# Output projection as three rounded passes with channels in partitions, in a fused attention and expert layer on one Trainium2 core

## The reference

```
x = x + attn(layernorm(x))
x = x + moe(layernorm(x))
```

## Time and profile before

| | |
|---|---|
| median of 3 runs | 872.1 us (870.09 to 872.9) |
| the profiled execution | 868.56 us |
| its span, first to last instruction | 866.8 us |
| mean granted TensorE clock | 0.997 |
| TensorE matmul busy | 846.0 us (98% of the span) |
| VectorE / ScalarE / GpSimd busy | 620.2 / 625.7 / 572.4 us |
| output projection on TensorE, 512 rows | 69.4 us |

### The profile page before, as it was taken

How to read it: one execution, slowest core, us unless ns; L and a number is a source line. 1 busy time by engine, 2 the same in 40 slices (tenths; PEclk the granted TensorE clock), 3 DMA queues, 4 the chain that set the end, 5 groups by cost and what they waited for, 6 DMA issues and landing times.

```text
span 866.8 us, 20127 instructions
## 1 busy us (share of the span) xinstructions
PE 846.0 (98%) x6535; PEld 670.2 (77%) x6535; DVE 620.2 (72%) x2348; ACT 625.7 (72%) x1639; POOL 572.4 (66%) x522
## 2 busy tenths in 40 slices
PE   8999999999999999999999999999998999999995
PEld 4677777777777777777777777777767999988884
DVE  6677787887777777878778778788787665545442
ACT  5877777877787777778877778777796776555552
POOL 5475576578657956775787569666748667555664
PEclk9999999999999999999999999999999999999998
DMA  7575550000000000000000000000011344333342
GB/s 197 207 285 211 235 161 2 1 26 8 7 8 26 1 7 9 24 8 1 21 13 7 5 29 1 8 7 26 8 26 44 48 56 67 44 51 48 50 53 26
DMA packets 44038, 44.69 MB, mean 52 GB/s; under 512 B 4112, under 2 KB 36240, under 8 KB 43936
## 3 DMA queue, kind: packets, MB, share of 16 engines
q0 software_dynamic: 16528, 26.03, 12.4%
q1 hardware_dynamic: 27120, 17.25, 7.1%
q10 hardware_dynamic: 288, 0.13, 0.1%
HBM read 15.28 MB, written 28.12 MB: 50 GB/s over the span
## 4 chain that ended last, share of the span: by engine, by line
PE 88%; DVE 4%; POOL 3%; issue 2%; ACT 2%; POOLq 0%; DVEq 0%; ACTq 0%
PE low_ps L1322 12%; PE low_ps L1309 9%; PE mid_ps L1244 7%; PE mid_ps L1246 7%; PE mid_ps L1245 7%; PE out_ps L1333 7%; PE top_ps L1309 7%; PE mid_ps L1295 6%; PE low_ps L1295 4%; PE low_ps L1534 4%; PE top_ps L1295 4%; POOL prob L408 2%; DVE prob L847 2%; PE out_ps L1509 2%; PE top_ps L1244 2%; PE top_ps L1246 2%
## 5 line engine op out<-in xcount | busy, mean ns | idle before, releaser
L408 POOL TENSOR_TENSOR prob<-prob,row_inv 128x512 f32<-128x512 f32 (+3 forms) x256 | 318.7, 1264 | 200.2 <-DVE row_inv L854 199.8
L588 ACT ACTIVATE prob<-prob,neg_max 128x256 f32<-128x256 f32 (+3 forms) x512 | 280.6, 550 | 7.8 <-DVE neg_max L847 0.9
L1322 PE MATMUL low_ps<-PT,v_sb 128*64 128x512 f32 (+3 forms) x1024 | 152.0, 439 | 0.3 <-ACT PT L594 0.3
L1322 PEld LDWEIGHTS low_ps<-PT,v_sb 128*64 128x64 f32 x1024 | 68.1, 136 | 92.1 <-issue 65.2
L859 DVE COPY PT<-low_ps 128x512 f32<-128x512 f32 (+1 forms) x128 | 104.1, 814 | 16.0 <-PE low_ps L1309 13.5
L599 ACT ACTIVATE v_sb<-mid_ps 128x512 f32<-128x512 f32 x64 | 38.3, 598 | 94.0 <-PE mid_ps L1246 93.8
L1160 DVE TENSOR_TENSOR prob<-mid_ps,prob 128x512 f32<-128x512 f32 x71 | 49.0, 691 | 78.1 <-PE mid_ps L1246 43.9
L847 DVE CUSTOM_DVE_ANT_0 prob<-mid_ps,mask 128x128 f32<-128x128 f32 (+1 forms) x256 | 93.5, 421 | 9.1 <-PE mid_ps L1295 4.9
L1309 PE MATMUL low_ps<-ident,prob 128*128 128x128 f32 x640 | 94.5, 278 | 2.0 <-POOL prob L408 0.5
L588 ACT ACTIVATION_READ_ACCUMULATOR prob<-prob,neg_max 128x1 f32 x512 | 95.7, 187 | 0.0
L594 ACT ACTIVATE PT<-top_ps 128x1024 f32<-128x1024 f32 x64 | 65.7, 1026 | 37.8 <-PE top_ps L1309 32.5
(11 more groups left out here) (253 smaller groups left out, 1872.2 us busy)
## 6 DMA issues: line engine op xcount, KB each, us to landing
routed_rows<-W_dn POOLq DMA_DIRECT2D x8, 2080.0 KB
X<-routed_rows SPq DMA_DIRECT2D x37, 65.0 KB
X<-routed_rows SPq DMA_DIRECT2D x17, 130.0 KB
X<-in_L_attn_x SPq DMA_DIRECT2D x8, 256.0 KB, 5.3
...
```

What stands on the lines that cost most here:

```text
L408: nc.gpsimd.tensor_tensor(p_pair(i), p_pair(i), row_inv[:, i, :].unsqueeze(2).to_broadcast([P, 2, P * (i + 1)]), ALU.mult).then_inc(S["nor ...
L588: nc.scalar.activation(p_at(i, h), p_at(i, h), ACT.Exp, bias=neg_max[:, i, h:h + 1], scale=-1.0, accum_out=row_sum[:, i, h:h + 1]).then_in ...
L1322: last = nc.tensor.matmul(y_ps[h * HD:(h + 1) * HD, j * P:T], v_sb[:, half, j, o + h * HD:o + (h + 1) * HD], PT[:, h, j, j:NT, :].rearrang ...
```

## The change

`project_out` turns its operands round. The weights are now a 128 x 128 piece of w_out and the moving operand is y with 512 tokens, so that out^T comes out with channels in partitions; and it is done in three rounded passes. For that:

- w_out is loaded into a buffer of its own and split once, near the start, into hi (ScalarE) and lo (VectorE).
- ScalarE's `y_copy` writes y's hi part, now between the two exponentials of block 3; VectorE makes the lo part (`y_lo`, new, one per step) after `t_copy(n, 1)`, which now stands ahead of `inv(n, 3)`; `project_out` waits for `y_lo_done`.
- Once a batch, ScalarE copies out^T (`post_out`, in k = 8), TensorE transposes it back in four products (`post_out`, in k = 1 of the next batch), and VectorE adds it to X from there (`post_x2`, now in k = 2).
- On VectorE, routing work changes places: `pre_stats` in k = 1 and `post_choose` in k = 5 go behind the step's last copy, `post_chosen` goes from behind it in k = 5 to ahead of `t_copy` in k = 6, and the cast to `row_i` goes from `post_weights` (k = 7) to `post_rows` (k = 6).
- At the end VectorE does `split_lo(4)`, `y_lo(63)`, `split_lo(2)`, `split_lo(6)`; `post_x2` of the last batch goes from `late(0)` to `late(1)`.
- Buffers: `y_sb`'s second use by the experts' part goes to `v_sb`, and the slots' weights and row numbers go to `wdT`.

```diff
-        Wo_sb = sb("Wo_sb", [P, NP, C])
+        Wo_sb = sb("Wo_sb", [P, 2, NP, C], F32R)
-        y_sb = sb("y_sb", [P, T])
+        y_sb = sb("y_sb", [P, T], F32R)
+        y_parts = [y_sb[:, :].rearrange("p (a n) -> p a n", a=2), xT_sb[:, 0, :, :]]
...
@@ ScalarE, step @@
-                    exps(n, 3)
+                    exp_head(n, 3, 0)
                 y_copy(n - 1)
+                if cur:
+                    exp_head(n, 3, 1)
...
+                if k == NP:
+                    post_out(n // NP - 1)
                 if cur:
                     t3_copy(n)
...
+            def post_out(b):
+                seen(act, S["out_ready"], NP * (b + 1))
+                seen(act, S["logits_ready"], b)
+                nc.scalar.activation(outT[:, :], out_ps[:, :], ACT.Copy).then_inc(S["outT_copied"], 1)
...
@@ VectorE @@
+            def y_lo(n):
+                seen(dve, S["y_copied"], n + 1)
+                seen(dve, S["out_ready"], n)
+                nc.vector.tensor_tensor(y_parts[1], y_ps.rearrange("p (a n) -> p a n", a=2), y_parts[0].bitcast(F32),
+                                        ALU.subtract).then_inc(S["y_lo_done"], 1)
...
-                if post is not None and k == 1:
+                if post is not None and k == 2:
                     post_x2(post)
-                if pre is not None and k == 1:
-                    pre_stats(pre)
...
-                if post is not None and k == 5:
-                    post_choose(post)
+                if post is not None and k == 6:
+                    post_chosen(post)
...
                 if cur:
+                    t_copy(n, 1)
+                y_lo(n - 1)
+                if cur:
                     inv(n, 3)
-                    t_copy(n, 1)
...
-            for e in (4, 2, 6):
+            split_lo(4)
+            y_lo(STEPS - 1)
+            for e in (2, 6):
                 split_lo(e)
...
@@ TensorE @@
             def project_out(n, pair):
-                seen(pe, S["y_copied"], n + 1)
+                seen(pe, S["y_lo_done"], n + 1)
                 if pair == 0:
-                    seen(pe, S["x2_done"], n // NP)
+                    seen(pe, S["outT_copied"], n // NP)
+                for k, (w, part) in enumerate(((0, 0), (1, 0), (0, 1))):
+                    last = nc.tensor.matmul(out_ps[:, :].rearrange("p (a n) -> p a n", a=2), Wo_sb[:, w, pair, :], y_parts[part],
+                                            start=(pair + k == 0), stop=(pair == NP - 1 and k == 2), skip_group_check=True)
+                last.then_inc(S["out_ready"], 1)
+
+            def post_out(b):
+                seen(pe, S["outT_copied"], b + 1)
...
                 for t in range(NT):
-                    last = nc.tensor.matmul(out_ps[:, t * P:(t + 1) * P], y_sb[:, t * P:(t + 1) * P], Wo_sb[:, pair, :],
-                                            start=(pair + t == 0), stop=(pair == NP - 1), skip_group_check=True)
-                last.then_inc(S["out_ready"], 1)
+                    last = nc.tensor.transpose(post_bank(b)[:, t * P:(t + 1) * P], outT[:, t * P:(t + 1) * P], ident[:, :])
+                last.then_inc(S["outT_ready"], 1)
```

More of the change, by code:

```diff
@@ L177, in layer @@
         hT_sb = [PT[:, a, 0, :, :].rearrange("p i q -> p (i q)") for a in range(2)]
-        eo_sb = [o[:, q * C:(q + 1) * C] for o in (prob[:, 4 * T:5 * T], y_sb) for q in range(RING)]
+        eo_sb = [o[:, q * C:(q + 1) * C] for o in (prob[:, 4 * T:5 * T], v_sb[:, 0, 0, :]) for q in range(RING)]
         w_up_sb = W_ffn[:, 0:2, :].rearrange("p a n -> p (a n)")
@@ L261, in layer @@
             "t0_ready", "t1_ready", "t2_ready", "t3_ready", "t0_copied", "t1_copied", "t2_copied", "t3_copied",
-            "y_ready", "y_copied", "out_ready",
+            "y_ready", "y_copied", "y_lo_done", "wo_hi", "wo_lo", "outT_copied", "outT_ready", "out_ready",
             "x2_done", "stats2", "rstd2", "xn2_done", "xn2T_ready", "xn2T_copied", "rows_copied",
@@ L291, in _ @@
             load_x(1)
-            sp.dma_start(Wo_sb[:, :, :], w_out.rearrange("(g d) c -> d g c", d=P)).then_inc(wo_in, 16)
+            sp.dma_start(Wo_in, w_out.rearrange("(g d) c -> d g c", d=P)).then_inc(wo_in, 16)
             for b in range(2, B):
@@ L614, in step @@
                     post_xn2T(post)
-                if post is not None and k == 5:
+                if post is not None and k == 6:
                     post_gap(post)
-                if post is not None and k == 6:
                     post_second(post)
@@ L674, in _ @@
             w_hi(Wv, 1, post_ps[:, :])
+            act.wait_ge(wo_in, 16)
+            nc.scalar.activation(Wo_sb[:, 0, :, :], Wo_in, ACT.Copy).then_inc(S["wo_hi"], 1)
             for bank, t in step0:
@@ L902, in step @@
                     w_lo(Wk, 1, 5, post_ps[:, :])
+                if pre is not None and k == 1:
+                    pre_stats(pre)
                 if post is not None and k == 2:
@@ L907, in step @@
                 if post is not None and k == 5:
-                    post_chosen(post)
+                    post_choose(post)
                 if post is not None and k == 6:
@@ L1018, in post_x2 @@
             def post_x2(b):
-                seen(dve, S["out_ready"], NP * (b + 1))
+                seen(dve, S["outT_ready"], b + 1)
                 xs = X[:, 4 * b:4 * b + 4, :].rearrange("p a c -> p (a c)")
-                nc.vector.tensor_tensor(xs, out_ps[:, :], xs, ALU.add).then_inc(S["x2_done"], 1)
+                nc.vector.tensor_tensor(xs, post_bank(b), xs, ALU.add).then_inc(S["x2_done"], 1)
             def post_stats(b):
@@ L1087, in post_rows @@
                 sig(nc.vector.tensor_reduce(row_f[:, :, :], picked[:, :, :, :], AX.X, ALU.add))
+                made(b, 17)
+                seen(dve, S["rows_written"], 16 * (K * NT * min(b, COUNTED) + FILLS + 1))
+                seen(dve, S["rows_late"], 16 * K * NT * (b - COUNTED))
+                sig(nc.vector.tensor_copy(row_i[:, :, :], row_f[:, :, :]))
             def post_weights(b):
@@ L1093, in post_weights @@
                 sig(nc.vector.tensor_scalar(weight[:, 1, :], gap_exp[:, :], 1.0, 1 / DEPTH_SCALE, ALU.add, ALU.mult))
-                made(b, 18)
+                made(b, 19)
                 sig(nc.vector.reciprocal(weight[:, 0, :], weight[:, 1, :]))
-                sig(nc.vector.tensor_copy(row_i[:, :, :], row_f[:, :, :]))
-                made(b, 19)
+                made(b, 20)
                 sig(nc.vector.tensor_tensor(weight[:, 1, :], gap_exp[:, :], weight[:, 0, :], ALU.mult))
@@ L1113, in _ @@
             w_lo(Wv, 1, 4, post_ps[:, :])
-            for i in (2, 0):
-                t_copy(0, i)
+            t_copy(0, 2)
+            dve.wait_ge(S["wo_hi"], 1)
+            nc.vector.tensor_tensor(Wo_sb[:, 1, :, :], Wo_in, Wo_sb[:, 0, :, :].bitcast(F32), ALU.subtract)\
+                .then_inc(S["wo_lo"], 1)
+            t_copy(0, 0)
             dve.wait_ge(consts, 18)
@@ L1246, in passes, with pre_T @@
                 return nc.tensor.matmul(dst, ws[0], vs[1], start=False, stop=stop, **kw)
-            def pre_T(b):
+            def pre_T(b, x2):
                 seen(pe, S["xn_done"], NT * b + NT)
+                seen(pe, S["x2_done"], x2)
                 seen(pe, S["routing"], ROUTING * (b - 3) + 14)
@@ L1352, in step @@
                         post_ranks(post)
+                    if k == 1:
+                        post_out(post)
                 if pre is not None and k == 3:
-                    pre_T(pre)
+                    pre_T(pre, m)
                 project_out(n - 1, (k - 1) % NP)
@@ L1565, in late @@
             def late(j):
+                if j == 1:
+                    post_out(B - 1)
                 if j == 4:
```

24 lines of the change are left out of this document (16 added, 8 removed).

## The result

The changed kernel takes **884.86 us** (median of 4 runs, 883.51 to 885.24) against 871.1 us (869.9 to 872.9) for the kernel before on the same chip: ratio 1.0151, 95% interval 1.0133 to 1.0168. It is slower by 1.5%: 10 us above the forecast of 874.9 us and outside the range, and +13.8 us where the sum said +2.8. The profiled execution took 885.24 us with a span of 883.4.

The account below looks back on a forecast made before the run. TensorE, busy 98% of the span, was taken as the bound, with a chain through y's low part nearly as long in each step. The terms summed to +2.8 us, from 872.1 giving 874.9 us; range 866 to 880.

Parts of the forecast that it names:

- 7 steps k = 6: Projection in the seventh step type: `post_ranks` hides part of the wait for y's low part; 0.80 for 0.96, -1.1 us.
- Step 62: A k = 6 step with `split_lo` and `post_chosen` ahead of block 1's copy; 0.3 us put for the delay.
- D: Time from block 1's transposes to block 2's in a step; forecast 2.81 us against 2.77 and 2.84 before.
- the low part as long as a `qk_lo`: VectorE's `y_lo` was taken to last as long as one of the two `qk_lo`, about 0.68 us.
- k = 1: Seven steps with out^T's four transposes ahead of the projection: 0.43 us for them, +0.32 each, +2.2 us.
- k = 3 and 4: 14 steps where `pre_T` or `post_xn2T` hides the wait for y's low part: 0.78 for 0.89, -1.6 us.
- steps 44 and 52: A 1.16 us `split_lo` ahead of block 1's copy delays y's low part; each loses 0.3 us, other products covering part.
- Rival 1: y's low part comes in time, so plain steps gain 0.23 us on average; sum -5.5, 866.6 us; chance 0.14.
- rival 2: As Rival 1, with the end and trailing work costing nothing: -8.3 us, with splits hidden -9.2, 862.9 us; chance 0.07.
- the end: After the loop, two `split_lo` stand behind `y_lo(63)`, so `tile_h(0)` is 1.9 us late: +1.9 us, or nothing.
- Batch end: ScalarE's copy of out^T, about 0.5 us, lies between `v_copy` and block 3's transposes: costs nothing.
- Longer work behind the last copy: `post_choose`, `pre_stats` and the cast may push the next maxima, nothing to 0.1 us per affected step: +0.3 us.

Follow-up runs that it names:

- e3: The kernel before with only `post_chosen` moved to its place in the changed kernel (k = 6, ahead of `inv(n, 3)`); ratio 1.0032 to the kernel before.
- e5: The changed kernel with `post_chosen` in k = 6 moved ahead of `inv(n, 0)` and `inv(n, 2)`; ratio 1.0060 to the kernel before.
- e1: The changed kernel with GpSimd's products of blocks 0 and 2 left out, but for one column per head, in routing k = 6 steps; ratio 1.0014.
- e4: The changed kernel with the last low part of y, `y_lo(63)`, behind all three `split_lo` at the end; ratio 1.0149 to the kernel before.
- e9: The changed kernel with `post_chosen` ahead of `inv(n, 0)` and no `y_lo`; the third pass repeats y's hi part; ratio 0.9953.
- e11: The changed kernel with `post_chosen` ahead of `inv(n, 0)`, earlier `y_copy` and `y_lo`, and `split_lo` and `w_lo` behind the step's last copy; ratio 1.0079.
- e12: The changed kernel with `post_choose` and `post_chosen` back where the kernel before has them, in k = 5; ratio 1.0061 to the kernel before.
- e2: The changed kernel with VectorE's order in every step: `y_lo`, `inv(n, 3)`, then block 1's copy; ratio 1.0086 to the kernel before.

## Why the prediction was wrong, point by point

**What failed: "7 steps k = 6: `post_ranks` covers only part; 0.80 for 0.96, -1.1 us".** Six of these steps cost +7.8 us, and with the seventh, step 62, it is +10.9; that is the miss. The step priced the projection in k = 6 and gave `post_chosen`, moved ahead of the copy there, no price; in step 62 it got "I put 0.3 us". Pricing it by its row would not have done either: its row in k = 5 is 0.19 us, taken beside an idle GpSimd, and beside GpSimd's product it is 1.34. e3, e5 and e1 show it: the move alone brings the 1.34 us, and without the collision (e5), or without GpSimd's work (e1), it is 0.19 again.

The Trainium skill, page "SBUF — State Buffer", section "Who interferes with whom", says that a VectorE instruction with two SBUF inputs contends with a GpSimd instruction that reads SBUF, that copies, casts and `tensor_scalar` can contend too, in modes that use both ports, and that whoever issues first holds the shared ports for its whole instruction. The trace agrees: 1.34 us against 0.19 for `chosen_bf`, while `y_lo` and `t_copy`, which read PSUM, kept their 0.68 beside GpSimd. The prediction did not weigh this rule against the moved instructions, although the trace of before had rows that show the effect: the cast in k = 7 (ns min/median/max: 204/388/391 before, 171/171/172 in its new place behind the last copy), and GpSimd's three products, 4.85 us for 3.89 beside the `split_lo` of step 62.

**Step 62, forecast +0.1 (the -0.16 of a step k = 6 and the +0.3), measured +3.1.** `split_lo` reads SBUF twice as well; there GpSimd's first two products took 3.13 us instead of 2.09 (the profile has the first one start 0.03 us ahead of `split_lo`, too near to tell which issued first), and one of the two compares of `post_chosen` took 1.41 us. TensorE waited 1.64 + 0.92 us, and in this execution its granted clock then stood at the lower level (columns as in the earlier trace rows):

```profile
655.25:657.25 2.00, 1.08 (x8) 0.81 (x9) 2.00 (x5) 1.72 (x2) 0.70 (x1) 1.00 0.00 0
657.25:658.50 1.25, 1.25 (x8) 1.24 (x7) 0.40 (x1) 0.00 (x0) 1.19 (x1) 0.53 0.00 0
658.50:660.70 2.20, 2.20 (x11) 1.90 (x9) 1.93 (x7) 0.00 (x0) 0.00 (x0) 0.50 0.03 7
```

0.50 is 1.2 GHz: the transposes of block 3 took 1.91 us where they take 1.09. In e4, with the same steps, the clock stayed at 1.00 there and step 62 took 12.39. So 1.2 of the 3.1 us is the clock. This is read from one execution; the other three have no trace, but a mean clock as low as this one's (0.994 to 0.995, e4's profiled one 0.996), so it may not be the only one.

**Step 47, not in the sum, +1.6.** The same hold, decided by 0.15 us. After, in step 47:

```profile
498.66 0.59 DVE L1129 TENSOR_SCALAR dest<-dest 128x8 f32<-128x8 f32 x1
...
499.57 1.10 DVE L1135 TENSOR_TENSOR weight<-gap_exp,weight 128x4 f32<-128x4 f32 x1
...
498.61 0.62 POOL L415 TENSOR_TENSOR prob<-prob,row_inv 128x256 f32<-128x256 f32 x1 [0.24 <-DVE row_inv L877]
499.18 1.47 POOL L415 TENSOR_TENSOR prob<-prob,row_inv 128x768 f32<-128x768 f32 x1
```

and in step 39, the same instructions:

```profile
416.19 0.15 DVE L1129 TENSOR_SCALAR dest<-dest 128x8 f32<-128x8 f32 x1
...
416.66 0.27 DVE L1135 TENSOR_TENSOR weight<-gap_exp,weight 128x4 f32<-128x4 f32 x1
...
416.29 0.61 POOL L415 TENSOR_TENSOR prob<-prob,row_inv 128x256 f32<-128x256 f32 x1 [0.24 <-DVE row_inv L877]
```

In step 39 `dest` starts 0.10 us ahead of GpSimd and `weight` slips in between two products; in step 47 `dest` comes 0.05 us behind and `weight` meets the long one. VectorE was late in step 47 because the second of two reciprocals waited for ScalarE's row sums of block 2, which were there at 498.55, 0.13 us behind the start of the first transposes (in step 38, 0.12 ahead of it). ScalarE was late in turn because VectorE's first maxima began 1.12 us behind the step's first scores, for 0.77 in the other steps looked at. Why they did, in all runs with `y_lo` (10.76 to 11.38 us for step 47), is open.

**What held.** D in plain steps (2.81 forecast, 2.84 measured) and with it their sum; the low part as long as a `qk_lo` (0.68); the weight load 0.06 us behind it for 0.05; k = 1 (+1.7 for +2.2) and the sign of k = 3 and 4 (-2.6 for -1.3, mis-sized by some 0.1 a step); steps 44 and 52; `tile_h(0)` late by 1.85 us for 1.9. Rival 1's and 2's premise, that the passes are worth 0.23 us a step once the low part is free, is e9's 0.25.

**Mis-sized: the end, +3.6 for +1.9.** `tile_h(0)` is 1.85 us later, and VectorE's last instruction comes 195.4 us behind it in both kernels: that is the forecast's term. The other 1.8 lie behind VectorE's last instruction, 10.5 us for 8.8 before; in the twelve experiments this stretch is 8.7 to 9.5 us in ten and 10.7 and 13.3 in two, one execution each, so it most likely belongs to the execution and not to the change. **Batch end, "nothing", measured +1.3** (k = 8, ScalarE's copy of out^T stands ahead of that of block 3); no run tested it. **Steps 1 and 2, not in the sum, +0.4**: `w_lo` in step 2 stands ahead of the copy too (e11). **Longer work behind the last copy, +0.3**: the steps behind `post_choose` take 9.79 us with it behind the last copy (e1) and 9.77 with it ahead (e12), so little of this term is seen.

The profiled executions differ by 16.7 us: 7.8 (k = 6) + 3.1 (step 62, the clock's 1.2 in it) + 1.6 (step 47) + 0.6 (all else of the loop) + 1.8 (`tile_h(0)`) + 1.8 (behind VectorE's last instruction). The medians differ by 13.8, since the profiled execution before lay 2.5 us under its median and the one after 0.4 above; which terms are smaller in the other executions is open.

Two sums of the prediction do not come out, and neither moves the forecast: for rival 2 the terms named give -7.7 and -8.6 us, not -8.3 and -9.2, and 14 steps of 0.11 us are 1.5 us, not 1.6.

No whole version of the changed kernel beats the kernel before; the best one, e5, is at 1.0060 (e12 at 1.0061), and the two edits that helped (e5 and e2) were not run together.
